# Layer 0 of a three-layer graph network: neighbour rows split into two fp32r parts, and small work moved between VectorE, GpSimd and ScalarE

## The reference, cut to what matters

```
h = max(layernorm(x), 0)                       # 100000 rows of 128
deg = segment_sum(1, dst); inv_deg = 1 / deg   # 150000 edges, one of them a self loop for each node

def sage(h, w_self, w_neigh, b):
    agg = segment_sum(h[src], dst) * inv_deg
    return h @ w_self + agg @ w_neigh + b

h = relu(sage(h, ws0, wn0, b0))                # 128 -> 256   layer 0
h = relu(sage(h, ws1, wn1, b1))                # 256 -> 256   layer 1
h = sage(h, ws2, wn2, b2)                      # 256 -> 128   layer 2
out = x + h
```

## Time and profile before

| | |
|---|---|
| Median of 3 runs | 3842.36 us (3839.69 to 3842.39) |
| The profiled execution | 3837.3 us, its span 3835.5 us |
| PE busy over the span | 3503.3 us, 91% |
| DVE busy | 3342.0 us, 87% |
| ACT busy | 3085.1 us, 80% |
| POOL busy | 2557.9 us, 67% |
| First pass (layer 0 and the first product of layer 1) | about 76 us to 2070 us |
| Second pass, third pass | to about 3145 us, to the end |

### The profile page before, as it was taken

How to read it: one execution, slowest core, us unless ns; L and a number is a source line. 1 busy time by engine, 2 the same in 40 slices (tenths; PEclk the granted TensorE clock), 3 DMA queues, 4 the chain that set the end, 5 groups by cost and what they waited for, 6 DMA issues and landing times. The chain is left out here.

```text
span 3835.5 us, 100978 instructions
## 1 busy us (share of the span) xinstructions
PE 3503.3 (91%) x22513; PEld 3162.4 (82%) x22513; DVE 3342.0 (87%) x9695; ACT 3085.1 (80%) x8036; POOL 2557.9 (67%) x3691
## 2 busy tenths in 40 slices
PE   1999999999999999999998999999999986777777
PEld 1888888888888888888887999998999976666666
DVE  7999999999999999999986888988988977777777
ACT  4888888888888888888886877878887867777777
POOL 2666666666666666666555777777777767777776
PEclk9999999999999999999999999999999986566555
DMA  2444444444444444444444888888888879999998
GB/s 75 138 143 143 144 142 144 143 144 144 144 143 144 143 142 143 142 143 144 141 145 143 247 245 247 249 248 244 247 246 246 249 216 263 262 262 266 262 265 249
DMA packets 828104, 727.99 MB, mean 190 GB/s; under 512 B 90198, under 2 KB 699614, under 8 KB 827918
## 3 DMA queue, kind: packets, MB, share of 16 engines
q1 hardware_dynamic: 642069, 570.14, 45.9%
q0 software_dynamic: 80336, 104.91, 11.5%
q10 hardware_dynamic: 105600, 51.92, 4.5%
HBM read 451.32 MB, written 361.23 MB: 212 GB/s over the span
## 5 line engine op out<-in xcount | busy, mean ns | idle before, releaser
L1445 PE MATMUL ps_out<-w_hi,hid_hi 128*128 128x512 f32 (+1 forms) x3136 | 1142.3, 364 | 27.3 <-DVE layer_mem L1336 24.7
L610 POOL DMA_INDIRECT loaded_rows<-in_x,gather_at x784 | 904.0, 1153 | 390.2 <-issue 241.7
L1445 PE MATMUL ps_out<-w_hi,hid_lo 128*128 128x512 f32 (+1 forms) x3136 | 1054.6, 336 | 0.0
L1445 PE MATMUL ps_out<-w_lo,hid_hi 128*128 128x512 f32 (+1 forms) x3136 | 1049.7, 335 | 0.0
L646 POOL DMA_INDIRECT layer_mem<-pq_rows,gather_at x784 | 788.2, 1005 | 273.2 <-issue 215.7
L1445 PEld LDWEIGHTS ps_out<-w_hi,hid_hi 128*128 128x128 f32 x3136 | 589.3, 188 | 135.4 <-issue 51.6
L659 POOL DMA_INDIRECT layer_mem<-zy_rows,gather_at x528 | 526.0, 996 | 182.3 <-issue 141.3
L1445 PEld LDWEIGHTS ps_out<-w_hi,hid_lo 128*128 128x128 f32 x3136 | 588.8, 188 | 68.8
L1445 PEld LDWEIGHTS ps_out<-w_lo,hid_hi 128*128 128x128 f32 x3136 | 591.1, 188 | 55.1
L750 ACT ACTIVATE layer_mem<-ps_hid,b_col 128x256 f32<-128x256 f32 x784 | 329.1, 470 | 211.4 <-PE ps_hid L1445 193.7
L837 ACT ACTIVATE layer_mem<-iota_row,triple_node 128x128 f32<-128x128 f32 x1056 | 337.3, 390 | 154.3 <-DVE layer_mem L1378 57.5
(11 more groups left out here) (172 smaller groups left out, 8817.2 us busy)
## 6 DMA issues: line engine op xcount, KB each, us to landing
pq_rows<-layer_mem SPq DMA_DIRECT2D x392, 512.0 KB, 3.2
loaded_rows<-pq_rows SPq DMA_DIRECT2D x392, 256.0 KB
zy_rows<-layer_mem SPq DMA_DIRECT2D x392, 256.0 KB
loaded_rows<-zy_rows SPq DMA_DIRECT2D x264, 192.0 KB, 4.1
layer_mem<-in_x SPq DMA_DIRECT2D x264, 192.0 KB
out_rows<-layer_mem ACTq DMA_DIRECT2D x264, 192.0 KB
loaded_rows<-in_x SPq DMA_DIRECT2D x392, 128.0 KB, 2.2
loaded_rows<-in_x,gather_at POOLq DMA_INDIRECT x784, 2.9
```

Of the source, the lines that this page charges most:

```text
L610: pool.indirect_dma_start(raw[s.slot][0:rows, 2 + j, :], None, table, bass.IndirectOffsetOnAxis(gather_at[s.slot][0:rows, j:j + 1], axis=0 ...
L1445: ins = nc.tensor.matmul(o, a, b, start=n == 0, stop=n == len(terms) - 1)
```

## The change

- **Neighbours in two parts.** ACT, after the norm (now neighbour tiles first, then own tiles), copies `h_nbr` of the pair rounded to fp32r into `halves[..., 0, :]` (one instruction, 128 x 260); DVE subtracts it from `h_nbr` into `halves[..., 1, :]` (128 x 260). For each tile PE makes one fp32r matmul of 260 columns (hi 130, lo 130) with `select` in place of the fp32 matmul. Each tile now has a PSUM bank of its own (`ps_agg` is 1024 wide), and DVE adds the second 128 columns in an instruction of its own (`rest_added`), which ACT's scaling waits for.
- **PSUM.** `ps_hid` becomes one bank in place of two; its product for pair t waits for `h1` of pair t-1.
- **Middle activations.** `hid_lo` is subtracted by POOL instead of DVE, as the first thing in POOL's step, for pair m-6 in its step m.
- **Shift.** POOL's two instructions and DVE's wait for them go; DVE makes `shift` in one `scalar_tensor_tensor`. `rstd` moves up ahead of the first half of the row.
- `layer1` uses parts of `halves` for its `nbr_hi` and `nbr_lo`, and its `row_sums` are the same four banks under other names.

```diff
@@ POOL, layer0_gathers
+                    v = first.back(6)
+                    if v.live():
+                        pool.wait_ge(L0.h1_hi_ready, v.n + 1)
+                        if v.has(2):
+                            pool.wait_ge(L0.dense_done, v.back(2).n + 1)
+                        pool.tensor_tensor(hid_lo[v.half][:, :, :], h1[v.half][:, :, :],
+                                           hid_hi[v.half][:, :, :].bitcast(FP32), ALU.subtract
+                                           ).then_inc(L0.h1_lo_ready, 1)
...
-                    t, u = first.back(2), first.back(3)
-                    if t.live():
-                        pool.wait_ge(L0.stats_done, t.n + 1)
-                        pool.tensor_tensor(minus_mean[t.half][:, :], moments[t.half][:, :, MEAN], minus_ones[:, :], ALU.mult
-                                           ).then_inc(L0.mean_turned, 1)
-                        pool.wait_ge(L0.mean_turned, t.n + 1)
-                        pool.wait_ge(L0.rstd_ready, t.n + 1)
...
-                        pool.tensor_tensor(shift[t.half][:, :], minus_mean[t.half][:, :], rstd[t.half][:, :], ALU.mult
-                                           ).then_inc(L0.shift_ready, 1)
+                    u = first.back(3)
@@ ACT, layer0
-                        act.wait_ge(L0.own_added, t.n + 1)
+                        act.wait_ge(L0.rest_added, t.n + 1)
...
+                        act.wait_ge(L0.nbr_normed, t.n + 1)
+                        if t.has(2):
+                            act.wait_ge(L0.summed, t.back(2).n + 1)
+                        act.activation(halves[t.half][:, :, 0, :], h_nbr[t.half][:, :, :], ACT.Copy
+                                       ).then_inc(L0.nbr_hi_ready, 1)
@@ DVE, layer0
-                v = first.back(5)
+                v = first.back(2)
                 if v.live():
 
-                    dve.wait_ge(L0.h1_hi_ready, v.n + 1)
+                    dve.wait_ge(L0.nbr_hi_ready, v.n + 1)
                     if v.has(2):
-                        dve.wait_ge(L0.dense_done, v.back(2).n + 1)
-                    dve.tensor_tensor(hid_lo[v.half][:, :, :], h1[v.half][:, :, :],
-                                      hid_hi[v.half][:, :, :].bitcast(FP32), ALU.subtract).then_inc(L0.h1_lo_ready, 1)
+                        dve.wait_ge(L0.summed, v.back(2).n + 1)
+                    dve.tensor_tensor(halves[v.half][:, :, 1, :], h_nbr[v.half][:, :, :],
+                                      halves[v.half][:, :, 0, :].bitcast(FP32), ALU.subtract).then_inc(L0.nbr_split, 1)
...
                 if u.live():
-                    dve.wait_ge(L0.std_ready, u.n + 1)
-                    if u.has(2):
-                        dve.wait_ge(L0.normed, u.back(2).n + 1)
-                    dve.reciprocal(rstd[u.half][:, :], std[u.half][:, :]).then_inc(L0.rstd_ready, 1)
+                    dve.wait_ge(L0.rstd_ready, u.n + 1)
+                    dve.scalar_tensor_tensor(shift[u.half][:, :], moments[u.half][:, :, MEAN], -1.0, rstd[u.half][:, :],
+                                             op0=ALU.mult, op1=ALU.mult).then_inc(L0.shift_ready, 1)
...
+                    dve.wait_ge(L0.own_added, s.n + 1)
+                    dve.tensor_tensor(agg[s.half][:, :, 0:D], agg[s.half][:, :, 0:D], lo_sums[:, :, 0:D], ALU.add
+                                      ).then_inc(L0.rest_added, 1)
@@ PE, layer0
-                    if t.has(2):
-                        pe.wait_ge(L0.h1_made, t.back(2).n + 1)
+                    if t.has(1):
+                        pe.wait_ge(L0.h1_made, t.back(1).n + 1)
...
-                    pe.wait_ge(L0.normed, t.n + 1)
+                    pe.wait_ge(L0.nbr_split, t.n + 1)
...
                     for j in range(2):
-                        last = nc.tensor.matmul(ps_agg[:, j * H:j * H + D + 2], select[t.half][:, j, :].bitcast(FP32),
-                                                h_nbr[t.half][:, j, :], start=True, stop=True)
+                        last = nc.tensor.matmul(agg_bank[j], select[t.half][:, j, :],
+                                                halves[t.half][:, j, :, :].rearrange("p t f -> p (t f)"),
+                                                start=True, stop=True)
```

More of the change, by code:

```diff
@@ L219, in build @@
         shift = [sb(f"shift{i}", [P, 4]) for i in range(2)]
-        minus_mean = [sb(f"minus_mean{i}", [P, 4]) for i in range(2)]
         h_own = [sb(f"h_own{i}", [P, 2, D]) for i in range(2)]
@@ L226, in build @@
         nbr = [part(2, H) for i in range(SLOTS)]
-        nbr_hi = [sb(f"nbr_hi{i}", [P, L1_SPLIT, H], FP32R) for i in range(2)]
-        nbr_lo = [sb(f"nbr_lo{i}", [P, L1_SPLIT, H], FP32R) for i in range(2)]
         gather_at = [sb(f"gather_at{i}", [P, SHARED], I32) for i in range(SLOTS)]
+        halves = [sb(f"halves{i}", [P, 2, 2, D + 2], FP32R) for i in range(2)]
         select = [sb(f"select{i}", [P, 2, P], FP32R) for i in range(2)]
+        nbr_hi, nbr_lo = ([t[:, :, :, :].rearrange("p j t f -> p (j t f)")[:, at:at + H].rearrange("p (j f) -> p j f", j=1)
+                           for t in halves] for at in (0, H))
         degree = [sb(f"degree{i}", [P, 2]) for i in range(2)]
@@ L298, in build @@
         b2_held = ps_out[1][:, 0:D]
-        strips = [ps_agg[:, D + 2 + j * H:D + 2 + j * H + TP] for j in range(2)]
+        strips = [ps_agg[:, j * 512 + 2 * (D + 2):j * 512 + 2 * (D + 2) + TP] for j in range(2)]
         w_loaded, bias_loaded = sem("w_loaded"), sem("bias_loaded")
@@ L630, in layer0_gathers @@
                 if not by_chunk:
-                    pipeline(pool, step, PAIRS, 3)
+                    pipeline(pool, step, PAIRS, 6)
                     return
@@ L749, in step @@
                         for m in range(2):
-                            last = act.activation(h1[t.half][:, m, :], ps_hid[t.half][:, m * PAIR:(m + 1) * PAIR],
+                            last = act.activation(h1[t.half][:, m, :], ps_hid[:, m * PAIR:(m + 1) * PAIR],
                                                   ACT.Relu, bias=b0_col[:, m:m + 1])
@@ L771, in step @@
                         if t.has(2):
-                            act.wait_ge(L0.summed, t.back(2).n + 1)
+                            act.wait_ge(L0.nbr_split, t.back(2).n + 1)
                             act.wait_ge(L0.turned, t.back(2).n + 1)
-                        for j in range(4):
-                            rows = h_own[t.half][:, j, :] if j < 2 else h_nbr[t.half][:, j - 2, 0:D]
-                            if general and j >= 2:
+                        for j in range(2, 4):
+                            rows = h_nbr[t.half][:, j - 2, 0:D]
+                            if general:
                                 last = act.activation(rows, raw[t.slot][:, j, :], ACT.Copy)
@@ L780, in step @@
                                                       bias=shift[t.half][:, j:j + 1], scale=rstd[t.half][:, j:j + 1])
+                        last.then_inc(L0.nbr_normed, 1)
+                        for j in range(2):
+                            last = act.activation(h_own[t.half][:, j, :], raw[t.slot][:, j, :], ACT.Relu,
+                                                  bias=shift[t.half][:, j:j + 1], scale=rstd[t.half][:, j:j + 1])
                         last.then_inc(L0.normed, 1)
+                        act.wait_ge(L0.nbr_normed, t.n + 1)
[3 more added lines that the diff above has]
+                                       ).then_inc(L0.nbr_hi_ready, 1)
                 return step
@@ L1202, in layer0 @@
                                       .to_broadcast(wide), ALU.is_equal).then_inc(L0.selected, 1)
+                u = first.back(1)
+                if u.live():
+                    dve.wait_ge(L0.std_ready, u.n + 1)
+                    if u.has(2):
+                        dve.wait_ge(L0.normed, u.back(2).n + 1)
+                    dve.reciprocal(rstd[u.half][:, :], std[u.half][:, :]).then_inc(L0.rstd_ready, 1)
                 t = first.back(6)
```

38 lines of the change are left out of this document (18 added, 20 removed).

## The result

The changed kernel takes 3858.02 us (median of 5 runs, 3855.73 to 3860.59), the kernel before 3842.38 (3839.69 to 3845.05, 6 runs). A sixth run of the changed kernel, 3996.18 us with a mean granted TensorE clock of 0.80 where the others have 0.92 or 0.93, is left out. The ratio is 1.0042, with a 95% interval of 1.0029 to 1.0056: slower by some 16 us, where 52 were forecast. The profiled execution is one of the five; its span is 3856.2 us.

The account below looks back on a forecast made before the run. PE was taken to bound the first pass at 5.03 us a step, with DVE taking over after the change. +42, -14 and +24 make +52 us: 3889 from the profiled 3837.3, 3894 as median; range 3858 to 3940.

Parts of the forecast that it names:

- PE's own step becomes 4.81: PE in the first pass: the shorter aggregation cuts its step from 5.03 us by 0.22.
- 86 us: First pass: the total saving over 392 steps if PE stayed the bound.
- First rival: First pass: PE's shorter step is paid out in full, 3756 us; chance 0.08.
- DVE's sum: DVE's work per first-pass step: +0.39 us net, 4.62 without a search round and 5.78 with one.
- the wait of the low sums: DVE's addition of the low sums waits for the end of `own_added`: +0.19 us a step.
- The ring of 9.66 us: Loop from `ps_hid` through ACT and DVE's `rstd` to `cat_lo`: two steps take at least 9.66 us, 4.83 each.
- +42: The 320 first-pass steps with search rounds go from 5.03 to 5.16 us each: 42 us more.
- The ring by way of `std`: The loop through `std` stretches two consecutive steps without a round by 0.42 us, twice in eight steps.
- The gathers: POOL's subtraction delays the gathers, so DVE's stats wait 0.06 us a step over 392 steps: +24 us.
- Steps without rounds: The 72 first-pass steps without search rounds go from 5.03 to 4.83 us each: -14 us.
- Balance, the second rival: First pass: rounds absorb the loop's stretch and the late gathers, -4 us, 3838; chance 0.18.
- The port: SBUF port pair shared by DVE and GpSimd: POOL's subtraction mostly misses `halves`; meeting it each step means over 4250 us.

Follow-up runs that it names:

- dve_pad: The changed kernel with one more DVE operation (128 x 128, two inputs) per step, behind the reciprocal of the degree: 3885.0 us, 1.0106 of the kernel before.
- early_lo: The changed kernel with DVE's subtraction into `halves` moved ahead of stats: 1.0304 of the kernel before.
- pool_pad: The changed kernel with one more POOL subtraction (128 x 256), waited for, between its `hid_lo` subtraction and the index copy: 4042.54 us, 1.0518 of the kernel before.
- dve_less: The changed kernel without DVE's addition of the low parts' sums, so its output is incomplete: 3831.0 us, 0.9976 of the kernel before.
- pe_less: The changed kernel without four of the hidden layer's twelve 256-column products (`w_lo` with `cat_hi`), output incomplete: 3832.82 us, 0.9980 of the kernel before.

## Why the prediction was right in its sign and wrong in its size

- *PE.* "PE's own step becomes 4.81": right, 4.81 and 4.83 measured, and its 86 us were not paid out. First rival out.
- *DVE's sum, the first step that failed.* "+0.39" was +0.20 (4.43 against 4.23): 0.15 too much for the wait of the low sums, 0.05 for `shift` and 0.02 for `halves`; some 0.03 elsewhere went the other way. I read the wait from `keys`, which stands directly behind `best_now`; here a reciprocal stands between. The ring of 9.66 us holds the same wait and the same `shift`, so it is 9.46 without them, and PE's own two steps, 9.64, are longer. With 9.64 the forecast's own formula gives (8 x 4.43 + 3 x 1.16 + 2 x (9.64 - 8.86))/8 = 5.06 us in place of 5.16; the eight steps shown above measure 5.09. `dve_pad` puts 0.15 back and gets 0.08 of it a step. In the forecast's sum the term "+42" came out at about +18.
- *The ring by way of `std`.* Forecast to stretch two steps in eight by 0.42, with DVE waiting for `std`. No wait for `std` is recorded on DVE in the changed kernel; `rstd` does start within 0.1 us of the end of `std` in 191 of 314 steps, so the two touch. But the ring ends at `ps_hid`, and there it has room: a released `ps_hid` starts 0.05 us behind `cat_lo` (above, in `early_lo`), and in the changed kernel it starts a median of 0.36 us behind it, under 0.15 in 9 of 314 steps. In steps without a stall it is PE's own length that counts, not the ring.
- *The gathers, the second step that failed.* "392 x 0.06 = +24": nothing came. The subtraction was longer than I took, yet the 0.80 from index copy to gather fell to a median of 0.34, and DVE waited for gathers 6.6 us in place of 19.6. `pool_pad` shows that late gathers do cost at 1.9 us of work ahead of the index copy; where between 1.3 and 1.9 that begins is not shown.
- *Steps without rounds.* "4.83, so -14": the last 40 steps took (2073.3 - 1882.4)/39 = 4.89, -5 us against 5.02 before.
- *Balance, the second rival*, came nearer with -4 us, where +16 were measured, but not by its reason: the rounds absorb nothing, since a wait of PE stands behind each of them. What `dve_less` and `pe_less` show is that neither DVE's sum nor PE's sets the step alone. Before, eight steps took DVE 8 x 4.23 + 3 x 1.16 = 37.3 us of PE's 40.2, and every round vanished in the 2.9. After, they are 38.9 of 38.6: a round of 1.16 goes through to PE as 0.67 of a longer step, and this takes back what the shorter aggregation gave: 3 x 0.67 = 2.0 us, and 0.1 in the other five steps, against 8 x 0.21 = 1.7 us. That is a loss of 0.4 us in eight steps, 0.05 a step, as `cat_lo` has it over the first 352 steps (5.10 against 5.05).
- *The port.* Priced by place, "it mostly misses": it did. `halves` lasts 0.40 to 0.43 us over all its 392 instances, and the changed kernel's keys copy keeps 168 ns. It hits as soon as the copy is moved to where the subtraction runs. By the Trainium skill (GPSIMD Engine Reference, section 3.1) the subtraction was an estimated 1.1 us and some dispatch; measured 1.30 us.

Terms of the sum, in us: steps with rounds +42 forecast, the 352 steps ahead of the last 40 measured +18 (352 x (5.104 - 5.051)); steps without -14, measured -5; gathers +24, in these none; second and third pass 0, about 1. The two terms that failed are 24 us each too much, and the steps without rounds gave 9 us less than forecast.

Open: why a round reaches PE as 0.67 us and not as more or less (no run gave `halves` a step more of room), why the gap ahead of the first gather closes, and why the changed versions' first pass is longer in the groups where the kernel before takes over 4240 us (`cat_lo` to 2137.1 against 2055.8 for the same kernel), when the kernel before's is not.

## What to carry to other kernels

When the bound engine is made shorter by work given to the next one, compare the sums over the whole pattern, rounds included: here 37.3 of 40.2 became 38.9 of 38.6, and what an uneven lump costs follows from the slack that is left, not from its mean. Look at buffers that are made and used in the same step; that a step more of room for them would even out the lumps is likely, and not tested here. A wait on an engine's own result costs by what stands between the two instructions: directly behind it stood 0.18 us, with one short instruction between 0.03 us.

## What the runs showed of the hardware that I had not expected

- A DVE copy of 88 x 8 lasts 136 to 167 ns in the kernel before and up to 1268 ns beside a GpSimd subtraction of 1.30 us; the same transfer as a reduction 144 to 150 ns beside it.
- From the start of GpSimd's index copy to that of the first gather it is a median of 0.80 us behind short work, 0.34 directly behind a subtraction of 1.30 us, and 0.81 in `pool_pad`, where a subtraction of 0.61 us and a wait for it stand ahead of the copy.
- The kernel before took 3837 to 3842 us in most groups and 4246 or 4284 in two; its first pass is as long in both (last `cat_lo` at 2054 to 2059 us), so the difference lies in the second and third passes.
